# Transformer block with causal attention: one decision on the score bound, read at the end, in place of one for each chunk

## The chip, the cores and the metric

The kernel runs on one core of one Trainium2 chip. The metric is the time of one execution on the device in microseconds (us), the median of three runs. Engines are named as in the profile: PE is TensorE's matmul, PEld its weight load, DVE is VectorE, ACT is ScalarE, POOL is GpSimd, SP is SyncE, which here issues all DMAs.

## What is computed

One pre-norm transformer block over 2048 tokens of width 256, in float32. The attention has 16 heads of width 16 and is causal; the second half is a linear layer with a routed low-rank addition (8 experts of rank 16, the best 2 of each token).

```python
def block(x):                       # x: 1, 2048, 256
    h = layernorm(x)
    Q, K, V = h @ Wq.T, h @ Wk.T, h @ Wv.T          # 16 heads of 16
    scores = Q @ K.T / 4
    scores = where(later key, -inf, scores)
    x = x + (softmax(scores) @ V) @ Wo.T
    h = layernorm(x)
    logits = h @ gate_w.T + gate_b
    top, at = top_k(logits, 2)
    gates = softmax(top)
    return x + h @ W.T + b + sum(gates * delta[at])  # delta = (h @ A.T) @ B.T for each expert
```

## The kernel before, in words

The tokens are cut into 16 tiles of 128 (`TILES`) and 4 chunks of 512 (`NCHUNK`, four tiles each). Attention goes through the chunks of queries in order. Within a chunk it goes through four quads of heads (`i`). The work is cut into 272 units (`UNITS`): a unit is the transposed scores of two heads (one bank for each) of one block of 128 keys against up to 512 queries, 1024 columns in all. ACT takes the exponential of a unit in one instruction (L846), without subtracting a row maximum; that is allowed as long as a bound on the scores holds. A chunk c has 8c+5 units for each quad, so the chunks have 20, 52, 84 and 116.

TensorE multiplies exponentials by values in groups (`GROUPS`, 160 of them): a group is one block of keys for the four heads of a quad, four matmuls side by side into the one bank `acc`, which is summed over all groups of the quad. After a quad's last group DVE copies `acc` out (`keep_sums`, L1067), and the next quad's first group waits for that copy (`acc_read`).

Three buffers limit how far the engines run apart. There are 3 score buffers (`BANKS`), so the scores of unit u wait for the exponential of u-3. There are 8 buffers for exponentials (`PROBS`), so the exponential of u waits until the values have used unit u-8 (`pv_done`, L845). There is one bank `aux` for all other matmuls.

The order is written out by hand in steps. Step s issues on PE the scores of units 2s and 2s+1 (L741), then a piece, then the groups due at this step (L758), then in chunk 0 a second piece. `steps_of_groups` sets when a group is due: two steps after its last unit, and the first group of a quad one step later still. A unit is at least partly above the diagonal in a quad's last five units; DVE clears the later keys there (`clear_later_keys`, L1062) after the exponential and before the values.

A piece (`place_pieces`) is one link of the chain of another tile: `turn_x`, `project_qk` and `project_v` prepare the tiles of the next chunk; `turn_sums`, `turn_back`, `o`, `turn_y`, `ffn`, `turn_gated` and `lora` finish a tile of an earlier chunk. Each waits for the reader of the piece before it, since all write `aux`. The last four tiles are finished after the loop (`TAIL_ORDER`).

The bound: for each chunk DVE squares the rounded queries and keys, two pieces (`norm_q`, `norm_k`, L624) sum the squares by head, DVE takes the maximum of each (L993) and decides in seven short instructions (`decide_bound`, L1006 to L1019) whether the scores stay small, written to `is_bounded[0, c]`. For chunk 0 that stands in `project_first_chunk`, ahead of the first scores; there PE also turns tile 4 (L604) only after `norm_read`.

At the start of each chunk PE, DVE and SP load `is_bounded[0, c]` into a register and branch on it. PE has the chunk's steps twice, once for each outcome, and so passes two branches in a row. With the inputs here the bound always holds, so the second copy and the shifts on DVE are always jumped over.

SP stores and reloads the split queries and keys of the next chunk through DRAM (`store_parts`, `load_queries`, `load_keys`): 16-bit halves, stacked by head. Before scores of a chunk start, PE waits for `stack_in`.

## Time and profile before

| what | value |
|---|---|
| median of 3 runs | 413.61 us (411.25 to 413.66) |
| the profiled execution, whole | 415.72 us |
| its span, first to last instruction | 413.9 us |
| mean granted clock of TensorE | 0.95 |
| PE busy | 363.4 us, 88% |
| ACT busy | 279.8 us, 68% |
| DVE busy | 213.3 us, 52% |
| bound for the chunk 0 decided, first scores | 22.9 us, 24.15 us |

The profile is of one execution. A busy time is the sum of an engine's instructions; an idle time stands at the instruction that ended it, with what released it ("issue" means that the profile shows nothing it waited for).
### The profile page before, as it was taken

The numbers are of one execution on the slowest core, as the hardware profiler recorded it, in microseconds if no ns is written. First come the engines' busy times: TensorE is split into PE (matmuls) and PEld (weight loads), VectorE is DVE, ScalarE is ACT, GpSimd is POOL, SyncE is SP. The second block draws the span as 40 slices with busy tenths as digits, with TensorE's granted clock in tenths as the row PEclk, the third lists the DMA queues.
The fourth block names the chain that finished last, engine by engine and source line by source line (L and its number), as shares of the span: only waits on it lengthen the run. The fifth ranks groups of instructions, "written<-read, shape, count | busy, mean of one in ns | idle before, by whom it ended". The sixth has DMA issues, their size and how long they took to land.

```text
span 413.9 us, 7036 instructions
## 1 busy us (share of the span) xinstructions
PE 363.4 (88%) x2558; PEld 142.1 (34%) x2558; DVE 213.3 (52%) x734; ACT 279.8 (68%) x317; POOL 47.8 (12%) x75
## 2 busy tenths in 40 slices
PE   7966975899998799999999979998997999797884
PEld 3544621445332254423323223233322323211542
DVE  4647565354766535555555444546446344402385
ACT  2524345767887777788788856888787588799121
POOL 5000100001011100011121111211121111100050
PEclk9988869899999999999999999999999899899896
DMA  6578335022350021261000000000000000000001
GB/s 197 159 253 258 82 103 157 18 60 78 89 169 13 3 53 51 74 194 52 14 1 15 13 5 13 2 14 0 14 13 2 13 2 13 14 0 4 3 1 51
DMA packets 29390, 23.51 MB, mean 57 GB/s; under 512 B 15392, under 2 KB 25888, under 8 KB 29344
## 3 DMA queue, kind: packets, MB, share of 16 engines
q1 hardware_dynamic: 29344, 22.91, 18.6%
q8 instruction: 28, 0.46, 0.5%
q14 instruction: 18, 0.15, 0.1%
HBM read 12.41 MB, written 10.49 MB: 55 GB/s over the span
## 4 chain that ended last, share of the span: by engine, by line
PE 63%; DVE 18%; issue 8%; ACT 8%; POOL 2%; DMA 1%; ACTq 0%; DVEq 0%
PE acc L758 23%; PE scores L741 12%; PE aux L612 7%; ACT probs L846 7%; PE aux L669 5%; PE aux L653 3%; PE aux L682 2%; DVE probs L1062 2%; PE aux L618 2%; PE aux L638 1%; DVE ffn L1109 1%; POOL exp_gap L1217 1%; DVE parts L977 1%; DVE gates L1137 1%; PE aux L661 1%
## 5 line engine op out<-in xcount | busy, mean ns | idle before, releaser
L846 ACT ACTIVATE probs<-scores 128x1024 f32<-128x1024 f32 x272 | 260.5, 1031 | 86.1 <-PE scores L741 74.9
L758 PE MATMUL acc<-probs,v_aug 128*32 128x512 f32 (+3 forms) x1280 | 149.5, 555 | 3.3 <-DVE probs L1062 2.4
L741 PE MATMUL scores<-q_stack,k_stack 64*128 64x512 f16 (+3 forms) x640 | 87.3, 357 | 15.6 <-issue 12.1
L741 PEld LDWEIGHTS scores<-q_stack,k_stack 64*128 64x128 f16 x640 | 21.1, 95 | 116.5 <-ACT probs L846 78.8
L1062 DVE TENSOR_TENSOR probs<-probs,masks_sb 128x512 f32<-128x512 f32 (+1 forms) x80 | 44.2, 579 | 23.9 <-ACT probs L846 23.3
L758 PEld LDWEIGHTS acc<-probs,v_aug 128*32 128x32 f32 x1280 | 31.8, 111 | 54.6 <-issue 34.9
L612 PE MATMUL aux<-xT,wqkv_sb 128*128 128x128 f32 x192 | 28.8, 311 | 1.0 <-DVE xT L964 1.0
L612 PEld LDWEIGHTS aux<-xT,wqkv_sb 128*128 128x128 f32 x192 | 26.4, 221 | 5.7 <-issue 3.2
L975 DVE CAST parts<-qk 128x512 f16<-128x512 f32 x12 | 5.1, 427 | 39.9 <-ACT qk L838 39.9
L1206 POOL TENSOR_TENSOR rstd<-ve,minus_half 128x1 f32<-128x1 f32 x12 | 7.3, 608 | 112.2 <-DVE ve L955 112.2
L669 PE MATMUL aux<-wffn_sb,yT 128*128 128x392 f32 x48 | 20.0, 543 | 0.0
L1211 POOL TENSOR_TENSOR rstd<-ve,minus_half 128x1 f32<-128x1 f32 x12 | 6.6, 549 | 106.3 <-DVE ve L1093 106.3
L1109 DVE COPY ffn<-aux 128x392 f32<-128x392 f32 x12 | 6.8, 567 | 22.8 <-PE aux L669 22.8
L1086 DVE TENSOR_TENSOR y<-aux,x_sb 128x256 f32<-128x256 f32 x12 | 5.1, 425 | 23.9 <-PE aux L653 23.9
L1217 POOL TENSOR_TENSOR exp_gap<-euler,top_gap 128x1 f32<-128x1 f32 x12 | 6.6, 550 | 90.3 <-DVE top_gap L1122 90.3
L1067 DVE COPY sums<-acc 128x512 f32<-128x512 f32 x16 | 11.0, 687 | 10.3 <-PE acc L758 10.2
L618 PE MATMUL aux<-wqkv_sb,xT 128*128 128x256 f32 x48 | 13.6, 405 | 1.2 <-ACT qk L838 1.0
L1159 DVE TENSOR_TENSOR result<-aux,yb 128x256 f32<-128x256 f32 x12 | 5.1, 425 | 17.7 <-PE aux L682 17.7
L1098 DVE TENSOR_SCALAR yln<-y,mv,rstd 128x256 f32<-128x256 f32 x12 | 9.7, 810 | 8.0 <-POOL rstd L1211 8.0
L653 PE MATMUL aux<-wo_sb,attn_t 128*128 128x256 f32 x48 | 13.6, 405 | 0.0
L838 ACT COPY qk<-aux 128x512 f32<-128x512 f32 x12 | 7.0, 585 | 9.4 <-PE aux L612 9.4
L676 PE MATMUL aux<-ident_sb,gated 128*128 128x128 f32 x12 | 3.9, 326 | 9.1 <-DVE attn_t L1080 8.2
(148 smaller groups left out, 328.1 us busy)
## 6 DMA issues: line engine op xcount, KB each, us to landing
q_stack<-q_dram SPq DMA_DIRECT2D x32, 128.0 KB, 2.8
k_stack<-k_dram SPq DMA_DIRECT2D x32, 128.0 KB, 2.8
qk_dram<-qk SPq DMA_DIRECT2D x12, 256.0 KB, 2.5
x_sb<-x SPq DMA_DIRECT2D x3, 512.0 KB, 6.8
q_dram<-parts SPq DMA_DIRECT2D x12, 128.0 KB, 2.0
k_dram<-parts SPq DMA_DIRECT2D x48, 32.0 KB, 1.9
out<-result SPq DMA_DIRECT2D x12, 128.0 KB, 1.7
qk_dram<-probs SPq DMA_DIRECT2D x4, 256.0 KB, 3.4
```

What stands on the lines that cost most here:

```text
L612: m = pe.matmul(aux[:, n * P:(n + 1) * P], wqkv_sb[:, k, col:col + P], xT[:, k, :], start=(k == 0), stop=(k == KH - 1))
L618: m = pe.matmul(aux[:, 0:D], xT[:, k, :], wqkv_sb[:, k, 2 * D:3 * D], start=(k == 0), stop=(k == KH - 1))
L653: m = pe.matmul(bank_of(g)[:, 0:D], w.attn_t[:, k, :], wo_sb[:, k, :], start=(k == 0), stop=(k == KH - 1))
L669: m = pe.matmul(bank_of(g)[:, 0:FFN], w.yT[:, k, :], wffn_sb[:, k, :], start=(k == 0), stop=(k == KH - 1), skip_group_check=True)
L741: m = pe.matmul(to, k_stack[row:row + STACK, kb // TPC, 2 * i + p, kb % TPC * P:(kb % TPC + 1) * P], q_stack[row:row + STACK, c % 2, 2 * i ...
L758: m = pe.matmul(acc[32 * hp:32 * hp + 32, lo:CHUNK], v_aug[:, kb, QUAD * i + hp, :], probs[:, u % PROBS, hp % 2, col:col + CHUNK - lo], st ...
L846: act.activation(probs[:, u % PROBS], scores[u % BANKS][:], ACT.Exp, scale=EXP_SCALE).then_inc(exp_done, 1)
L1062: dve.tensor_tensor(tile, tile, mask, ALU.min).then_inc(causal_done, 1)
L1067: dve.tensor_copy(sums[:, c % 3, i, :], acc[:]).then_inc(acc_read, 1)
L1098: dve.tensor_scalar(w.yln, w.y, w.mv2[:, 0:1], w.rstd2, ALU.subtract, ALU.mult).then_inc(yln_ready, 1)
L1109: dve.tensor_copy(w.ffn, bank_of(g)[:, 0:FFN]).then_inc(ffn_ready, 1)
L1217: pool.tensor_tensor(w.exp_gap, euler[:], w.top_gap, ALU.pow).then_inc(gap_exp, 1)
```

## The change

There is one decision for the whole kernel instead of four. `norm_q` and `norm_k` of chunk 0 become pieces like the others, behind the projections of chunk 1; the decision is made once, after `norm_k` of chunk 3. The steps run without any load or branch. At the very end PE, ACT, DVE, POOL and SP each load the one result and branch: if the bound does not hold, a general path in compact loops computes the attention again and overwrites the output. With the inputs here it is jumped over.

A group of values is now due three steps after its last unit, and the extra step ahead of a quad's first group is gone. `squares` has two buffers. The mask loaded from DRAM has one plane instead of two, and the semaphores and buffers of the old general path are gone.

```diff
-        s = max(s, (last_unit(g) + 4) // 2 + (1 if g.first else 0))
+        s = max(s, (last_unit(g) + 6) // 2)
...
-            pre += [("norm_q", c + 1), ("norm_k", c + 1)]
             if c == 0:
                 pre.remove(("turn_x", TPC))
+                pre += [("norm_q", 0), ("norm_k", 0)]
+            pre += [("norm_q", c + 1), ("norm_k", c + 1)]
...
-        squares = sb("squares", [P, 2 * KH, CHUNK], BF16)
+        squares = sb("squares", [P, 2, 2 * KH, CHUNK], BF16)
...
                 pe.wait_ge(consts_in, 16 * 2)
-                pe.wait_ge(squared, 2 * KH)
-                pe.wait_ge(first_qk32_ready, 2)
-                for a in range(2):
-                    sum_squares(0, a, first_banks[a])
-                pe.wait_ge(norm_read, 1)
+                pe.wait_ge(first_qk32_ready, 1)
                 turn_x(TPC)
...
             pe.wait_ge(ones_set, 1)
-            for c in range(NCHUNK):
-                if c == 1:
+            for s in range(STEPS):
+                if s == FIRST_STEP[1]:
                     pe.wait_ge(post_weights_in, 16 * 5)
-                pe.wait_ge(bound_step, BOUND_STEPS * (c + 1))
-                bounded = pe.value_load(is_bounded[0:1, c:c + 1], min_val=0, max_val=1)
-                with pe.If(bounded == 1):
-                    for s in range(FIRST_STEP[c], FIRST_STEP[c + 1]):
-                        step(s, False)
-                with pe.If(bounded == 0):
-                    pe.wait_ge(gen_loaded[c], 16 * QUAD * (2 * c + 5))
-                    if c > 0:
-                        pe.wait_ge(exp_done, FIRST_UNIT[c])
-                    pe.wait_ge(*bank_read(*PIECE_BEFORE[PIECE_AT[FIRST_STEP[c], 0]]))
-                    row_maxima(c)
-                    for s in range(FIRST_STEP[c], FIRST_STEP[c + 1]):
-                        step(s, True)
-            for s in range(QK_STEPS, STEPS):
-                step(s, False)
+                step(s)
             pe.wait_ge(exp_done, len(UNITS))
...
+            pe.wait_ge(bound_step, BOUND_STEPS)
+            bounded = pe.value_load(is_bounded[0:1, 0:1], min_val=0, max_val=1)
+            with pe.If(bounded == 0):
+                general()
...
                 normalise_x(TPC)
-                for a in range(2):
-                    read_norm(0, a, first_banks[a])
-                decide_bound(0)
                 store_xT(TPC)
...
             def norm_k(c):
-                read_norm(c, 1, aux[:])
-                decide_bound(c)
+                read_norm(c, 1)
+                if c == NCHUNK - 1:
+                    decide_bound()
...
             for t in range(TPC):
                 store_result(TILES - TPC + t)
+            sp.wait_ge(bound_step, BOUND_STEPS)
+            bounded = sp.value_load(is_bounded[0:1, 0:1], min_val=0, max_val=1)
+            with sp.If(bounded == 0):
+                general()
             for b in range(2):
```

SP and DVE lose their loads and branches in the loop in the same way, and ACT and POOL gain the load and branch at their end.

The order on PE where chunk 0 begins. Before (`aux<-squares` are the sums of squares, `aux<-ident_sb,xln` turns tile 4, `scores<-q_stack,k_stack` are the first units):

```order
L590 MATMUL scores<-wqkv_sb,probs 128x256 x8
L624 MATMUL aux<-squares,head_sum_sb 16x512 x2
L624 MATMUL acc<-squares,head_sum_sb 16x512 x2
L604 MATMUL aux<-ident_sb,xln 128x128 x2
L778 TENSOR_LOAD is_bounded
L778 ISA x2
L779 COMPARE_AND_BRANCH
L741 MATMUL scores<-q_stack,k_stack 128x512 x4
L612 MATMUL aux<-xT,wqkv_sb 128x128 x8
```

and now:

```order
L578 MATMUL scores<-wqkv_sb,probs 128x256 x8
L588 MATMUL aux<-ident_sb,xln 128x128 x2
L696 MATMUL scores<-q_stack,k_stack 128x512 x4
L596 MATMUL aux<-xT,wqkv_sb 128x128 x8
```

The sums of squares, the load and the branch are gone from between the first chunk's values projection and the first scores. The sums stand in steps 5 and 6 of chunk 0 instead.

The order on PE where chunk 0 ends. Before, the copy for a bound that holds ends with:

```order
L741 MATMUL scores<-q_stack,k_stack 128x384 x2
L741 MATMUL scores<-q_stack,k_stack 128x128 x2
L741 MATMUL scores<-q_stack,k_stack 128x256 x4
L758 MATMUL acc<-probs,v_aug 32x256 x4
L779 UNCONDITIONAL_BRANCH
L782 COMPARE_AND_BRANCH
```

and, behind 130 rows of the other copy, chunk 1 begins:

```order
L782 UNCONDITIONAL_BRANCH
L778 TENSOR_LOAD is_bounded
L778 ISA x2
L779 COMPARE_AND_BRANCH
L741 MATMUL scores<-q_stack,k_stack 128x512 x4
L604 MATMUL aux<-ident_sb,xln 128x128 x2
L741 MATMUL scores<-q_stack,k_stack 128x512 x4
L612 MATMUL aux<-xT,wqkv_sb 128x128 x8
L758 MATMUL acc<-probs,v_aug 32x512 x4
```

Now the two chunks stand in a row:

```order
L696 MATMUL scores<-q_stack,k_stack 128x384 x2
L696 MATMUL scores<-q_stack,k_stack 128x128 x2
L696 MATMUL scores<-q_stack,k_stack 128x256 x4
L713 MATMUL acc<-probs,v_aug 32x384 x4
L713 MATMUL acc<-probs,v_aug 32x128 x4
L696 MATMUL scores<-q_stack,k_stack 128x512 x4
L588 MATMUL aux<-ident_sb,xln 128x128 x2
L713 MATMUL acc<-probs,v_aug 32x256 x4
L696 MATMUL scores<-q_stack,k_stack 128x512 x4
L596 MATMUL aux<-xT,wqkv_sb 128x128 x8
L713 MATMUL acc<-probs,v_aug 32x512 x4
```

No load and no branch is left there, and `acc<-probs,v_aug` has moved back: the last group of one quad (32x256), which stood in step 9, now stands in step 10, and the four groups of the next quad, which stood together in step 11, are spread over steps 11 and 12.

The order on PE at the last scores. Before, up to the fourth pair of branches:

```order
L741 MATMUL scores<-q_stack,k_stack 128x384 x2
L741 MATMUL scores<-q_stack,k_stack 128x128 x2
L741 MATMUL scores<-q_stack,k_stack 128x256 x4
L758 MATMUL acc<-probs,v_aug 32x512 x4
L779 UNCONDITIONAL_BRANCH
L782 COMPARE_AND_BRANCH
```

with, behind the jump, the last four groups:

```order
L758 MATMUL acc<-probs,v_aug 32x512 x4
L758 MATMUL acc<-probs,v_aug 32x384 x4
L758 MATMUL acc<-probs,v_aug 32x128 x4
L758 MATMUL acc<-probs,v_aug 32x256 x4
```

and now:

```order
L696 MATMUL scores<-q_stack,k_stack 128x384 x2
L696 MATMUL scores<-q_stack,k_stack 128x128 x2
L696 MATMUL scores<-q_stack,k_stack 128x256 x4
L713 MATMUL acc<-probs,v_aug 32x512 x12
L713 MATMUL acc<-probs,v_aug 32x384 x4
L713 MATMUL acc<-probs,v_aug 32x128 x4
L713 MATMUL acc<-probs,v_aug 32x256 x4
```

Three full groups (12 matmuls) instead of two stand behind the last scores, and no branch is between them.

## Rows read from the trace of the kernel before

**Rows 1.** The page's first part: busy us, share of the span, instructions

```profile
PE 363.4 (88%) x2558; PEld 142.1 (34%) x2558; DVE 213.3 (52%) x734; ACT 279.8 (68%) x317; POOL 47.8 (12%) x75
```

**Rows 2.** The waits: engine, line, waited for: us in all, times, longest us

```profile
PE scores L741 <- issue: 12.1, 4, 4.1
...
ACT probs L846 <- PE acc L758: 10.9, 7, 2.9
```

**Rows 3.** Stretches of the span, by engine

```profile
core 0: us, PE busy (x) PEld busy (x) DVE busy (x) ACT busy (x) POOL busy (x), PEclk, DMA share, GB/s
143.00:242.00 99.00, 96.68 (x735) 35.77 (x730) 53.07 (x183) 81.26 (x88) 11.62 (x19) 1.00 0.18 49
246.00:353.00 107.00, 100.83 (x702) 31.02 (x700) 50.80 (x193) 83.96 (x88) 16.22 (x26) 0.97 0.03 8
...
24.60:28.00 3.40, 3.40 (x17) 3.21 (x16) 0.00 (x0) 1.92 (x2) 0.00 (x0) 0.51 0.80 240
...
72.40:75.80 3.40, 3.40 (x16) 2.39 (x15) 1.09 (x5) 2.46 (x3) 0.54 (x1) 0.51 0.01 2
...
141.70:145.10 3.40, 3.40 (x26) 1.55 (x27) 1.09 (x5) 2.98 (x4) 0.55 (x1) 1.00 0.00 0
...
246.40:249.80 3.40, 3.40 (x12) 0.86 (x10) 1.02 (x7) 1.43 (x2) 0.00 (x0) 0.50 0.00 0
```

**Rows 4.** The source lines of the load, the two branches and DVE's branch

```profile
L778 PEldq TENSOR_LOAD <-is_bounded x4: 298/312/500, 23.0 to 244.6; - x4
...
L779 PEldq COMPARE_BRANCH  x4: 80/80/95, 23.9 to 245.2; - x4
...
L782 PEldq COMPARE_BRANCH  x4: 3294/3485/4160, 66.4 to 379.6; - x4
...
L1190 DVEq COMPARE_BRANCH  x4: 56/59/67, 24.7 to 242.3; - x4
```

**Rows 5.** Timeline, 12 to 32 us, and the landing times of k_stack

```profile
17.03 1.97 SPq L457 DMA_DIRECT2D k_stack<-k_dram  x4
...
20.01 0.41 DVE L959 TENSOR_SCALAR xln<-x_sb,mv,rstd 128x256 f32<-128x256 f32 x1 [0.67 <-POOL rstd L1206]
...
21.07 0.44 PE L604 MATMUL aux<-ident_sb,xln 128*128 128x128 f32 x2 [0.72 <-DVE norms L993]
...
24.15 0.71 PE L741 MATMUL scores<-q_stack,k_stack 64*128 64x512 f16 x4 [2.65 <-issue]
...
DMA to landing us min/median/max: 2.7/2.9/3.8
```

**Rows 6.** Timeline: the first rows after the three chunk boundaries

```profile
72.00 2.85 ACT L846 ACTIVATE probs<-scores 128x1024 f32<-128x1024 f32 x3 [3.30 <-PE scores L741]
...
142.12 3.85 ACT L846 ACTIVATE probs<-scores 128x1024 f32<-128x1024 f32 x4 [2.59 <-PE scores L741]
...
245.46 0.61 PE L741 MATMUL scores<-q_stack,k_stack 64*128 64x512 f16 x4 [2.86 <-issue]
```

**Rows 7.** Timeline, 372 to 392 us: the last groups of values

```profile
379.89 1.06 PE L758 MATMUL acc<-probs,v_aug 128*32 128x512 f32 x8
...
382.29 0.69 DVE L1062 TENSOR_TENSOR probs<-probs,masks_sb 128x512 f32<-128x512 f32 x1 [0.22 <-ACT probs L846]
...
383.36 4.67 PE L758 MATMUL acc<-probs,v_aug 128*32 128x512 f32 x32 [2.40 <-DVE probs L1062]
```

**Rows 8.** All the sums of squares, from the groups by line

```profile
L624 PE MATMUL aux<-squares,head_sum_sb 128*16 128x512 bf16 x14 | 5.0, 447 | 2.9 <-DVE v_aug L988 2.9
```

**Rows 9.** Timeline: an exponential that waited for values, and the projection behind it

```profile
103.45 1.02 ACT L846 ACTIVATE probs<-scores 128x1024 f32<-128x1024 f32 x1 [1.72 <-PE acc L758]
...
105.01 1.13 PE L618 MATMUL aux<-wqkv_sb,xT 128*128 128x256 f32 x4 [0.28 <-ACT qk L838]
```

**Rows 10.** The page's fifth part: the copy of the sums

```profile
L1067 DVE COPY sums<-acc 128x512 f32<-128x512 f32 x16 | 11.0, 687 | 10.3 <-PE acc L758 10.2
```

**Rows 11.** Timeline, 388 to 414 us: the last stores

```profile
409.40 2.71 SPq L484 DMA_DIRECT2D out<-k_stack  x4
```

More of the change, by code:

```diff
@@ L505, in store_shifts @@
[L505 to L513 removed]
+                sp.dma_start(gen_band, band).then_inc(gen_band_in, 16)
@@ L1202, in _ @@
+            bounded = dve.value_load(is_bounded[0:1, 0:1], min_val=0, max_val=1)
+            with dve.If(bounded == 0):
+                general()
         @block.gpsimd
@@ L1274 @@
         "expert_ids": np.broadcast_to(np.arange(E, dtype=np.float32)[None], (P, E)).copy(),
-        "ones": np.ones((1, NQUAD, S), np.float32),
+        "band": np.where(np.arange(2 * S - P)[None, :] - (S - P) <= row[:, None], BIG, -BIG).astype(np.float32),
     }
```

568 lines of the change are left out of this document (287 added, 281 removed).

## Prediction

> **What bounds the kernel now.** I read the busy shares first: PE is busy for 88% of the span, ACT for 68% [rows 1]. A share is a mean over stages, so the stretches come next. Between 143 and 242 us PE is busy for 96.68 of 99.00 us and ACT for 81.26; between 246 and 353 us PE is busy for 100.83 of 107.00 [rows 3]. There the order of work on PE is the time: whatever leaves PE, or fills an idle time of PE, moves the end. Then the waits: the longest idle time of PE is 12.1 us before L741, in only 4 places, released by "issue" [rows 2], so nothing computed was being waited for. The timeline puts them at the first scores of the four chunks: 2.65 us at 24.15 [rows 5], 2.86 at 245.46 [rows 6] and, behind the other two, ACT stands idle for 3.30 and 2.59 us waiting for scores [rows 6].
>
> What is being done there, the source lines tell [rows 4]. The branch at a chunk's start, which falls through (L779), takes 80 ns. The branch that jumps over the copy for the general path (L782) takes 3294 to 4160 ns, four times: after chunks 0, 1, 2 and also after chunk 3. Its last one starts at 379.6, so it ends at about 383; the values that wait at 383.36 behind 2.40 us of idle time [rows 7] are put down to DVE's last clearing, which ended at 382.98. But the first group there needs only earlier units, and groups before it ended at 380.95. I take these 2.40 us as a fifth boundary, made by the branch. DVE's branch over its compact body takes 59 ns [rows 4]: it is the length of the jump that costs, not the branch.
>
> The Trainium skill has two rules on this, and they disagree on what the change gives. Advanced Engine Details and Errata (Control Flow Timing) gives some 108 ns for a compare-and-branch; by that the five places would give back half a microsecond in all. Runtime: NRT & Kernel Launch (Instruction fetch mechanics) says that a taken branch to a target outside the fetched pages stalls for the fetch; by that the places give back what L782 takes. The trace agrees with the second for L782 and with the first for L779 and L1190.
>
> **The change part by part.** The sum is made against the profiled execution, 415.72 us with a span of 413.9; the median of the runs, 413.61, is 2.1 us lower, and I apply the same difference to it.
>
> Head. Before, PE turned tile 4 at 21.07 after the norms, then waited for the bound and the load, and began at 24.15 [rows 5]. Now the tile can be turned when xln is written, 20.42, and the scores wait for k_stack: four DMAs issued from 17.03 to 19.00, the last at about 18.6, landing 2.9 us later at 21.4 (at worst 3.8, 22.4) [rows 5]. First scores at 21.5: gain 2.6, between 1.7 and 3.1.
>
> Boundaries. After chunk 0, ACT was idle 3.30 us; PE's idle time was longer (4.1, the longest in rows 2), but the third and fourth unit's scores wait for exponentials there, so I take ACT's: 3.3. After chunk 1 ACT's 2.59, of which I take 2.5; after chunk 2 PE's 2.86, taken as 2.9 [rows 6]. Sum 8.7. Lower bound 5: at each, a wait for an exponential or for DVE's clearing might stand behind the branch for 1.2 us. Upper bound 9.5. What is late next: the scores of chunk 1 need reloaded keys, whose DMAs shift earlier with the head, since they start from the projection of tile 7.
>
> End. A full group takes 1.06 us [rows 7]. From 379.89 on, PE now has three full groups (383.07) and the short ones, 384, 128 and 256 columns or 1.5 groups, 1.6 us: 384.7. The last clearing ends at 382.98, in time for the last group. Before, the same point was 383.36 + 4.67 = 388.03 [rows 7]. Gain 3.3, between 2.4 and 3.6. The lag of three steps adds a group behind the last scores, but it fills time in which PE waited for the last exponentials anyway.
>
> Clock. Right after the first and the third boundary PE ran 3.40 us without a gap at a granted clock of 0.5; after the second it did not fall [rows 3]. At full clock the same work takes 1.7 us. Without the idle times ahead of them, at least 3.30 and 2.86 us, I expect both stretches to go: 2 x 1.5 = 3.0, between 0 and 3.4. The stretch at 24.60 [rows 3] follows a head in which PE still does little, so I keep it. TensorE: Matmul & The Clock Gate (the HAM clock gate) in the Trainium skill ties the half clock to idleness before it; the rows agree for two boundaries and not for the second.
>
> Norm pieces. Four matmuls of sums move from the head into steps 5 and 6 of chunk 0. All 14 take 5.0 us [rows 8], so four take 1.4, on PE's path: cost 1.4, between 0 (chunk 0 is full of small waits that may cover them) and 3.
>
> Values a step later. PE's work is the same; three things change. (a) The exponential of u waits for the values of u-8. Counted from the tables, the group that it needs stands in the same step as its own scores for 8 units before and for 61 now. (b) A quad's first group stands right behind the last group of the one before, and `acc` must be copied between: 0.69 us [rows 10] plus some 0.2 of waiting on both sides, while scores (0.61 [rows 6]) and mostly a piece (0.44 or more [rows 5]) cover it; 15 times. (c) Waits of the values for fresh exponentials and clearings go, but none of the rows that I read shows one on PE besides the end's. For (a) the trace has the pattern: ACT waited 7 times, 10.9 us [rows 2], once for 1.72 us at 103.45, and PE behind it, at a projection that needs an ACT copy queued behind that very exponential, lost 0.28 us [rows 9]. ACT has 18 us of slack in 99 [rows 3]. I take 1.2 us for all of (a) to (c), between -1 and 6.
>
> Loop body on DVE and SP. Three decisions of seven short instructions and the loads leave DVE, which is idle half the time [rows 1]: 0, between -0.5 and 0. The extra fill of the small mask: 0.
>
> New end. After the last store SP loads and branches. The load to the branch took 23.0 to 24.0 on PE [rows 4], and the stores are issued until 412.1 [rows 11], so SP is through at 413.2, before the last landing at 413.9; the general paths are now short enough to jump like DVE's. Cost 0, at most 3.3, the least that a long jump takes [rows 4], if one engine's at the end is one.
>
> Sum: -2.6 - 8.7 - 3.3 - 3.0 + 1.4 + 1.2 = -15.0. That is 400.7 us for a profiled execution and 398.6 for the median.
>
> **The rivals.**
> Serial ACT and PE (the slower side). If each of the 53 new same-step dependencies cost PE what ACT waited less the one exponential it is ahead, 10.9/7 - 1.02 [rows 2, 9] = 0.54 us, that is 28.6 us: 398.6 + 28.6 = 427. It decides from 0.28 us each, where it eats the whole gain. For it: the last quad has 11 such steps in a row, and ACT is the bound there. Against it: the loss of 0.28 behind a wait of 1.72, and that two steps of PE (groups, scores, pieces) with even the shortest pieces take 2 x (0.61 + 1.06 + 0.44) = 4.2 us, and the loop of two exponentials, half the scores, a piece and a group takes 2 x 1.02 + 0.3 + 0.44 + 1.06 = 3.8.
> The boundaries were cover. What stood behind the branches (exponentials, clearings, landing keys) takes half of it, and the half clock comes elsewhere: -2.6 - 5 - 2.4 + 0 + 1.4 + 1.2 = -7.4, so 406. For it: the scores behind a boundary do need the last exponentials ahead of it, and the clock did not follow the gaps at the second boundary.
> The stall stays, since the change doesn't remove what made it: gain only the head less the norms and the lag, about 0: 413.6. The skill's 108 ns rule would be this case. Against it: L782's 3.3 to 4.2 us are in the records.
>
> **How the numbers follow.** Forecast 0.68, half the gain 0.18, no change 0.08, serial 0.06. A measurement of this kernel tells about 1% from no change, 4.1 us. Faster by over 1% (below 409.5) takes the forecast, and all but a little of the second: 0.85. Within 1%: 0.10. Slower: 0.05. The range: the terms' bounds in the good direction, not all at once, give 394; the second rival's 406 is near the other end. I take 394 to 405.5.
>
> **What would show it.** Right: no PE idle time of over 2 us between 30 and 360 us at a chunk's first scores; first scores at about 21.5; full clock behind the boundaries of chunks 1 and 3; "ACT waits for PE acc" grows from 7 to tens of times while PE's idle time does not; the last value group ends about 15 us before its 388.03; the tail from there to the end stays 26 us long. Wrong: PE idle at L758 released by DVE's copy of the sums; PE waiting for ACT at scores in the last quad, with exponentials no longer back to back; a long gap of one engine at the end; chunk 1's first scores released by a DMA.

## The result, and the profile after

The changed kernel takes 393.45 us, the median of four runs (392.62 to 394.21). The kernel before takes 412.71, the median of the three runs above and one more beside the changed kernel. The ratio is 0.9536, with a 95% interval from 0.9495 to 0.9576, so the change takes off 19.3 us. Runs more than 1.5% above the fastest of their kernel are left out of a ratio, which concerns three of ten runs in two of the experiments below. Measured once more later, next to three other kernels, it took 394.35 us (six runs, 393.13 to 395.14) against 413.08: ratio 0.9539 [0.9499, 0.9580].

Forecast were 398.6 us, in a range from 394.0 to 405.5. The direction is right; the time lies 0.55 us outside the range, on the fast side. The gain was foretold as 15.0 us and is 19.3. The later measurement, 394.35, lies just inside the range, so the 0.55 us alone would say little; that the gain is 4 to 5 us larger than the sum stands in both.

The profiled execution of the changed kernel took 394.21 us, with a span of 392.4 and a mean granted clock of 0.988. Two lines of its page, from the first part, which answers to [rows 1], and the second:

```profile
PE 350.8 (89%) x2558; PEld 135.4 (34%) x2558; DVE 210.3 (54%) x711; ACT 279.7 (71%) x317; POOL 47.6 (12%) x75
...
PEclk8999999999999999999999999999999999999997
```

The number of matmuls is what it was, 2558, but PE is busy for 350.8 us in place of 363.4. This is the first line to stop at: an engine that does the same work in 12.6 us less did it at another speed. ACT's busy time did not move (279.7 against 279.8).

The waits (engine, line, what it waited for: us in all, times, longest us), which answer to [rows 2]:

```profile
ACT probs L814 <- PE acc L713: 31.3, 39, 1.9
...
PE aux L657 <- DVE attn_t L1027: 9.7, 11, 1.9
...
PE aux L602 <- ACT qk L806: 6.6, 5, 2.5
```

"PE scores <- issue: 12.1, 4, 4.1" is gone; 0.51 us of it is left, at the first scores of the kernel. ACT's waits for values grew from 7 to 39 places and from 10.9 to 31.3 us, as the prediction said they would. PE pays for some of them at L602, in `project_v`: three waits of 1.14 us, in chunks 1 and 2, where one of 0.28 stood before. The other two waits there are in chunk 0, and the longest, 2.5 us, is missing in the changed kernel's second profile.

The loop, cut at the first exponential of each chunk and at the end of the last values, first before and then after. The columns are the stretch, its length, the busy time of each engine (with instructions), PEclk, DMA share and GB/s:

```profile
core 0: us, PE busy (x) PEld busy (x) DVE busy (x) ACT busy (x) POOL busy (x), PEclk, DMA share, GB/s
24.60:72.00 47.40, 34.62 (x252) 19.98 (x250) 27.36 (x72) 21.45 (x24) 2.00 (x3) 0.82 0.57 172
72.00:142.10 70.10, 63.82 (x513) 27.33 (x511) 40.23 (x118) 52.12 (x56) 6.28 (x10) 0.98 0.22 63
142.10:245.90 103.80, 98.62 (x746) 36.27 (x744) 55.03 (x185) 82.91 (x89) 11.62 (x19) 1.00 0.17 47
245.90:388.00 142.10, 130.18 (x915) 38.27 (x913) 57.79 (x208) 110.50 (x116) 16.22 (x26) 0.95 0.02 8
```

```profile
23.65:63.75 40.10, 28.71 (x250) 16.05 (x248) 26.36 (x66) 21.28 (x25) 2.55 (x4) 1.00 0.65 192
63.75:130.60 66.85, 62.77 (x517) 25.86 (x519) 39.49 (x112) 52.06 (x58) 6.28 (x10) 1.00 0.27 76
130.60:233.65 103.05, 98.94 (x744) 36.33 (x737) 55.54 (x185) 83.04 (x90) 11.61 (x19) 1.00 0.17 47
233.65:366.30 132.65, 124.21 (x921) 36.36 (x919) 58.38 (x209) 110.51 (x117) 16.23 (x26) 1.00 0.02 8
```

Between these two executions (415.72 and 394.21) the head gives 0.9 us, chunk 0 7.3, chunk 1 3.3, chunk 2 0.7, chunk 3 9.5, and the tail from the last values to the end takes 0.2 more, 26.1. In each stretch the busy time of PE and its remainder, the idle time, can be read apart. In chunk 3 idle time falls by 3.5 us (11.92 to 8.44) and busy time by 6.0 (130.18 to 124.21), with a PEclk of 0.95 before and 1.00 after. That is the half clock, and it is the larger part: the kernel before ran at 0.50 in four stretches of chunk 3, at 246.4 [rows 3], at 321.5 (shown further down) and in these two, and the changed kernel in none.

```profile
355.60:359.00 3.40, 3.40 (x22) 1.18 (x14) 0.43 (x2) 1.30 (x2) 0.00 (x0) 0.50 0.02 5
382.90:386.30 3.40, 2.94 (x12) 0.66 (x12) 0.09 (x1) 0.00 (x0) 0.00 (x0) 0.50 0.03 5
```

Rows of the timeline after (start, duration, engine, line, what, and in brackets the idle time before it and what ended it), which answer to [rows 5], [rows 9] and [rows 7]:

```profile
22.30 0.41 PE L588 MATMUL aux<-ident_sb,xln 128*128 128x128 f32 x2 [1.18 <-DVE xln L936]
23.22 0.61 PE L696 MATMUL scores<-q_stack,k_stack 64*128 64x512 f16 x4 [0.51 <-issue]
...
68.36 1.02 ACT L814 ACTIVATE probs<-scores 128x1024 f32<-128x1024 f32 x1 [1.72 <-PE acc L713]
...
69.92 1.13 PE L602 MATMUL aux<-wqkv_sb,xT 128*128 128x256 f32 x4 [1.14 <-ACT qk L806]
...
351.57 13.02 ACT L814 ACTIVATE probs<-scores 128x1024 f32<-128x1024 f32 x14
...
362.21 4.08 PE L713 MATMUL acc<-probs,v_aug 128*32 128x512 f32 x48
```

The bound no longer stands ahead of the first scores; they begin 0.9 us earlier than before (24.15) here, and at 21.75 in the changed kernel's second profile. Near the end ACT runs 14 exponentials back to back, the last ones of the loop among them. The last values follow without an idle time where 2.40 us stood [rows 7], and end at 366.29, that is 26.1 us before the end, while before it was 25.9. At 68.36 and 69.92 is the new chain: an exponential 1.72 us late, ACT's copy queued behind it, and PE's projection 1.14 us late behind the copy. The same pattern before cost PE 0.28 us [rows 9].

The new end (L761 loads the flag, L762 branches):

```profile
L762 PEldq COMPARE_BRANCH  x1: 233/233/233, 389.3 to 389.3; - x1
...
L761 PEldq TENSOR_LOAD <-is_bounded x1: 720/720/720, 388.2 to 388.2; - x1
```

It lies beside the last stores, and the tail is 0.2 us longer than before.

### The profile page after: what moved, and what is told of

It reads as the page before. It is cut to its first block, busy times and chain, and to the rows that moved or that the text cites. A ratio compares the mean times of both kernels' runs of the same rounds, so it can differ in the third digit from the quotient of the medians.

```text
span 392.4 us, 6977 instructions
## 1 busy us (share of the span) xinstructions
PE 350.8 (89%) x2558; PEld 135.4 (34%) x2558; DVE 210.3 (54%) x711; ACT 279.7 (71%) x317; POOL 47.6 (12%) x75
## 4 chain that ended last, share of the span: by engine, by line
PE 61%; DVE 20%; SPq 5%; issue 5%; ACT 4%; DMA 3%; POOL 2%; DVEq 0%; ACTq 0%
PE acc L713 24%; PE scores L696 11%; PE aux L596 5%; PE aux L651 4%; PE aux L637 3%; ACT probs L814 3%; PE aux L662 2%; PE aux L602 2%; DVE ffn L1055 2%; DVE probs L1010 2%; POOL exp_gap L1216 2%; DVE gates L1083 2%; PE aux L623 1%; DMA wqkv_sb<-wqkv 1%; SPq L455 1%
## 5 line engine op out<-in xcount | busy, mean ns | idle before, releaser
L713 PE MATMUL acc<-probs,v_aug 128*32 128x512 f32 (+3 forms) x1280 | 146.5, 538 | 0.8 <-DVE sums L1015 0.8
L696 PE MATMUL scores<-q_stack,k_stack 64*128 64x512 f16 (+3 forms) x640 | 85.1, 349 | 1.8 <-issue 0.5
L1010 DVE TENSOR_TENSOR probs<-probs,mask_sb 128x512 f32<-128x512 f32 (+1 forms) x80 | 44.8, 578 | 25.3 <-ACT probs L814 25.1
L713 PEld LDWEIGHTS acc<-probs,v_aug 128*32 128x32 f32 x1280 | 29.1, 108 | 41.5 <-issue 23.9
L596 PE MATMUL aux<-xT,wqkv_sb 128*128 128x128 f32 x192 | 24.6, 281 | 0.7 <-DVE xT L941 0.7
L596 PEld LDWEIGHTS aux<-xT,wqkv_sb 128*128 128x128 f32 x192 | 22.3, 191 | 4.7 <-issue 2.8
L602 PE MATMUL aux<-wqkv_sb,xT 128*128 128x256 f32 x48 | 13.6, 405 | 6.8 <-ACT qk L806 6.6
L651 PE MATMUL aux<-wffn_sb,yT 128*128 128x392 f32 x48 | 19.0, 518 | 0.0
```

Source lines behind the costliest of these rows:

```text
L596: m = pe.matmul(aux[:, n * P:(n + 1) * P], wqkv_sb[:, k, col:col + P], xT[:, k, :], start=(k == 0), stop=(k == KH - 1))
L602: m = pe.matmul(aux[:, 0:D], xT[:, k, :], wqkv_sb[:, k, 2 * D:3 * D], start=(k == 0), stop=(k == KH - 1))
L651: m = pe.matmul(w.bank[:, 0:FFN], w.yT[:, k, :], wffn_sb[:, k, :], start=(k == 0), stop=(k == KH - 1), skip_group_check=True)
L696: m = pe.matmul(scores[u % BANKS][:, j, col:col + n], k_stack[row:row + STACK, kb // TPC, 2 * i + p, kb % TPC * P:(kb % TPC + 1) * P], q_s ...
L713: m = pe.matmul(acc[32 * hp:32 * hp + 32, lo:CHUNK], v_aug[:, kb, QUAD * i + hp, :], probs[:, u % PROBS, hp % 2, col:col + CHUNK - lo], st ...
L1010: dve.tensor_tensor(tile, tile, mask, ALU.min).then_inc(causal_done, 1)
```

## The experiments

Twelve measurements were made, in three sets of four, each set next to new runs of the kernel before. Theory 1 is the prediction's mechanism: the long jump at four chunk ends, the idle time it makes on PE, and the half clock that follows that idle time. The question was which of its terms was too small.

### The branches alone

From the kernel before, the branches, the loads of the flag and all the general path are taken out; the bound is still decided per chunk, chunk 0's ahead of the first scores, and the values stand at their old step.

```diff
-                bounded = pe.value_load(is_bounded[0:1, c:c + 1], min_val=0, max_val=1)
-                with pe.If(bounded == 1):
-                    for s in range(FIRST_STEP[c], FIRST_STEP[c + 1]):
-                        step(s, False)
-                with pe.If(bounded == 0):
...
+                for s in range(FIRST_STEP[c], FIRST_STEP[c + 1]):
+                    step(s, False)
```

> The kernel before without any load or branch in the loop; the bound is still decided for each chunk, and PE still waits for chunk 0's decision. The general path is left out, and never ran. Theory 1 (the far jumps cost their own time and bring half-clock stretches with them, and that is nearly all of the gain): 396 to 399 us, half-clock time in the span down from 41 us to under 20. Rival (the values a step later bring the part that the forecast missed): 400 to 402, half-clock stretches in the last two chunks stay. Rival (the jumps only cover waits): 406 or more.

Measured: 396.69 us (395.19 to 397.02), ratio 0.9592 [0.9527, 0.9657] to a before of 412.65. So 16.0 of the 19.3 us go with the loads and branches. The load and branch ahead of chunk 0's first scores are among them: the first exponential starts at 23.45 in place of 24.60, so 1.1 us of what the prediction called the head are in this number. Its stretches:

```profile
23.45:66.06 42.61, 33.89 (x254) 19.77 (x252) 26.84 (x75) 21.34 (x24) 2.55 (x4) 0.84 0.64 187
66.06:132.36 66.30, 61.90 (x510) 26.09 (x509) 40.41 (x119) 52.10 (x58) 6.27 (x10) 1.00 0.27 72
132.36:233.20 100.84, 98.53 (x746) 36.24 (x744) 54.93 (x186) 82.90 (x90) 11.61 (x19) 1.00 0.17 48
233.20:369.00 135.80, 126.24 (x915) 37.15 (x913) 58.32 (x210) 110.53 (x116) 16.21 (x26) 0.97 0.02 8
```

Chunk 1 gives 3.8 us and chunk 2 3.0, where the terms said 4.0 (2.5 and half of the clock's 3.0) and 2.9. Chunk 0 gives 4.8 where 3.3 was said, chunk 3 6.3 where 4.8 was said. The expectation's number for half clock missed: 26 us are left in the span (2 x (1 - 0.967) x 394.9). Chunk 0 still has a PEclk of 0.84, though there is no jump in it.

### The values a step later, alone

```diff
-        s = max(s, (last_unit(g) + 4) // 2 + (1 if g.first else 0))
+        s = max(s, (last_unit(g) + 6) // 2)
```

> The kernel before with the new due times of the groups only (three steps, no extra step before a quad's first group). Theory 1: the same or slower by up to 3 us (411 to 416), since ACT now waits for values in the same step 61 times. Rival (the later values bring the missed part): faster by 4 us or more, under 409.

Measured, on the kernel before: 413.96 us (ten runs, 409.64 to 416.77; 412.48 for the seven that the ratio takes), ratio 0.9991 [0.9940, 1.0042]. Alone it does nothing that can be told in the time. Its profile has both sides of it: chunk 2 takes 106.0 us in place of 103.8, and chunk 3 takes 138.1 in place of 142.1, with 3.4 us at half clock where the kernel before had 13.7.

### Everything but the later values

The same line the other way round, in the changed kernel.

> The changed kernel with the old due times of the groups. Theory 1: 391 to 394.5 us, no slower than the changed kernel's 393.45, because the branches are what went. Rival (later values): 397 to 400, with half-clock stretches back around 320 and 355 us.

Measured: 394.13 us (393.17 to 394.80), ratio 0.9545 [0.9481, 0.9608]. By these medians the later values are worth 0.7 us, within the spread. Against the kernel without branches, this one differs by the head and the place of the sums of squares: 396.69 - 394.13 = 2.6 us, where the prediction's two terms were 2.6 and 1.4 the other way, 1.2 net; and since 1.1 us of the head went with the branches, only 0.1 was left to expect. The two intervals overlap widely, so the difference is not resolved.

### The kernel before, once more

A control: the unchanged kernel under a name of its own, for the granted clock of more executions than one.

> The kernel before once more, for the granted clock of several executions. Theory 1: mean clock 0.94 to 0.96 in all of them, against 0.98 to 0.99 of the changed kernel. Rival (the clock of the one profiled execution was bad luck): some executions of before at 0.97 or more, and their times lower by the half of the stretches that they lack.

Measured: 413.83 us (ten runs, 409.34 to 417.73; 413.65 for the seven that the ratio takes), ratio 1.0000 [0.9955, 1.0044]. The medians of this kernel in the five measurements on record lie between 412.65 and 413.83, its single runs between 409.34 and 417.73. The expectation on the clock was too narrow: the mean clocks of the ten executions run from 0.943 to 0.975, and the fastest execution is the one at 0.975. In the 46 executions of this kernel that ran beside the experiments the median is 0.962, which is 31 us of half clock, so the profile that the prediction rests on, with 0.950 and 41 us, is one of the low ones.

### Four far jumps put back

The changed kernel, in which PE loads a constant flag at the end of each chunk and jumps over 700 matmuls, which never run.

```diff
+SKIPPED = 700
...
+                if s in FIRST_STEP[1:]:
+                    flag = pe.value_load(flag_cell[0:1, 0:1], min_val=0, max_val=1)
+                    with pe.If(flag == 0):
+                        for _ in range(SKIPPED):
+                            pe.matmul(aux[:, 0:P], ...)
```

> The changed kernel with a load and a branch on PE alone put back ahead of the first step of chunks 1, 2 and 3 and ahead of the last values; each branch jumps over 700 matmuls that never run, and there is no wait for a bound. Theory 1 (the far jump is the price): PE idle 2.2 to 3.5 us at each of the four places, branch records over 3 us, half-clock stretches back behind one or more of them; 404 to 409 us. Rival (the load and the wait for the bound were the price, not the jump): under 398.

Measured: 415.12 us (ten runs, 412.20 to 417.81), ratio 1.0036 [0.9999, 1.0072]. The whole gain is gone; theory 1 had expected 404 to 409 and was too low by 6 us at least.

### Four near jumps

The same with 20 matmuls to jump over in place of 700.

> The same, but each branch jumps over 20 matmuls. Theory 1: branch records of 0.05 to 0.25 us, PE loses at most the load, 0 to 1 us at each place: 393.5 to 397 us. Rival (any branch or load drains PE's queue and costs the same): as far_jumps, 404 or more.

Measured: 395.41 us (393.40 to 397.86), ratio 0.9548 [0.9483, 0.9612], 2.0 us above the changed kernel's 393.45, 1.1 above its 394.35, and as theory 1 said. In the profiles the near jumps cost 0.3 us up to the last values (345.20 against 344.95 in the changed kernel's second profile, shown last); 1.0 us more lies at the very end, a tail of 27.1 us in place of 26.1, with the far jumps too, and no run shows why. The source line of the branch (ns min/median/max), and the row that sums four stretches from the first exponential to the last values, for the far and then for the near jumps:

```profile
L760 PEldq COMPARE_BRANCH  x4: 3274/3582/4152, 62.8 to 379.3; - x4
...
sum 363.90, PE 326.22 PEld 118.42 DVE 180.05 ACT 267.40 POOL 36.71; mean PE 81.55 PEld 29.60 DVE 45.01 ACT 66.85 POOL 9.18
```

```profile
L760 PEldq COMPARE_BRANCH  x4: 205/210/243, 63.5 to 363.7; - x4
...
sum 345.20, PE 316.08 PEld 114.88 DVE 179.77 ACT 266.99 POOL 36.70; mean PE 79.02 PEld 28.72 DVE 44.94 ACT 66.75 POOL 9.18
```

This is the cleanest reading of the case, since the two programs differ in nothing that runs. The far one takes 18.7 us more between these points. Its matmuls are the same, and PE is busy for 10.1 us more (326.22 - 316.08); idle time accounts for the other 8.6 (37.7 against 29.1). So a far jump costs 4.7 us in these two executions: 2.1 of idle PE, and 2.5 of matmuls that run slower. The sum of 4.7 holds, since the medians (415.12 and 395.41) give 4.9. The split is less sure, for not all of the half clock lies behind a jump. The far kernel has two stretches of 3.4 us at half clock ahead of its first jump that the near one lacks, and one at 322.8 with no jump near. Behind the jumps themselves stand 13.7 us at half clock, after the first (66.8), the second and the third, and none after the fourth; they are worth at most half of that, 1.7 us a jump. The second and the third:

```profile
138.50:141.90 3.40, 3.40 (x15) 0.67 (x15) 1.09 (x5) 1.64 (x2) 0.55 (x1) 0.50 0.00 0
244.30:251.10 6.80, 5.57 (x16) 1.54 (x16) 1.45 (x10) 1.02 (x1) 0.14 (x1) 0.50 0.01 2
```

Chunks 1 to 3 alone take 15.2 us longer with far jumps, 8.1 of it idle time and 7.1 slower matmuls. Over all executions of the two kernels the mean clocks give 33 and 13 us at half clock (medians), so at most 10 of the 19.7 us between the medians are the clock's. About half and half is what the runs bear out. The timeline shows both at the first jump: 4.13 us of idle time, and the four score matmuls behind it take 1.04 us in place of 0.61.

```profile
67.07 1.04 PE L698 MATMUL scores<-q_stack,k_stack 64*128 64x512 f16 x4 [4.13 <-issue]
```

The Trainium skill, Runtime: NRT & Kernel Launch (Instruction fetch mechanics), has a taken branch to a target outside the fetched pages wait for the fetch. These records agree: 0.21 us near, 3.3 to 4.2 us far, with the same flag and the same branch. The DMA queue of the instructions agrees too, first with far and then with near jumps (packets, MB, share of 16 engines):

```profile
q8 instruction: 28, 0.46, 0.5%
```

```profile
q8 instruction: 22, 0.36, 0.4%
```

In the far trace one packet of 16384 bytes starts inside each of the four branch records, 0.9 to 1.7 us after its start (64.4, 135.0, 242.8 and 380.2 us). In the near trace one of the four records has a packet beside it, and that branch took 0.21 us all the same.

### Matmuls that fill the idle time

The kernel before, with twelve unused matmuls of 512 columns issued at the end of each chunk, just ahead of the jump.

```diff
+                    for _ in range(FILL):
+                        pe.matmul(aux[:], ident_sb[:].bitcast(BF16)[:, 0:P], k_stack[:, 0, 0, :].bitcast(BF16),
+                                  start=True, stop=True)
```

> The kernel before with 12 matmuls of 512 columns into the unused bank aux ahead of each of its four far jumps (2.6 us of work at full clock that nobody reads; a wait for the last piece's reader is added), so that PE is busy while its sequencer is stalled. Theory 1 (the idle time brings the half clock): PE's idle time at the boundaries shrinks to under 1.5 us, the half-clock stretches right behind them go, and the time falls by 2 to 5 us though the jumps stay: 408 to 411. Rival (the clock falls whatever PE does there): 412 to 416.

Measured: 410.19 us (408.74 to 411.67), ratio 0.9916 [0.9883, 0.9949]: 2.9 us less, with more work in it. The jumps still take 3.3 to 4.05 us each. Two of its stretches, chunks 1 and 3:

```profile
69.05:139.50 70.45, 64.93 (x524) 27.41 (x523) 40.23 (x118) 52.09 (x56) 6.29 (x10) 1.00 0.23 63
...
244.85:381.80 136.95, 127.39 (x926) 38.04 (x925) 57.69 (x208) 110.29 (x116) 16.21 (x26) 0.99 0.03 8
```

PEclk rises from 0.98 to 1.00 in chunk 1 and from 0.95 to 0.99 in chunk 3, and chunk 3 is 5.1 us shorter though its record holds 11 matmuls more. The stretches at half clock that stood behind the first, the third and the fourth jump of the kernel before are gone, with the jumps still there. So at these places PE's idle time brought the half clock, and not the branch as such. The 5.1 us of chunk 3 are not all the filling's, since the stretch at 355.6 is missing too and stood behind no jump; and chunk 2, which had no half clock to lose, takes 1.5 us more for it.

### Nine buffers for exponentials

The changed kernel with `PROBS` 9 in place of 8 (the squares of chunk 0 move into memory that is free then). With nine, the exponential of u waits for values of an earlier step.

```diff
-PROBS = 8
+PROBS = 9
```

> The changed kernel with nine buffers for exponentials instead of eight (the squares of chunk 0 move into the third buffer of the sums to make room), so that no exponential needs values of its own step. Theory 1 (the lag's cost is the same-step dependency, paid in chunks 1 and 2): ACT's waits for values fall from 31 us to under 5, chunk 2 gets 1.5 to 2.5 us shorter, 391 to 392.5 us in all. Rival (the cost is the copy between a quad's last and the next one's first group): 393 to 394.5, as the changed kernel.

Measured: 390.27 us (388.32 to 392.02), ratio 0.9423 [0.9367, 0.9480], a little better than expected in the whole; chunk 2 gained less than the 1.5 to 2.5 us expected. The waits, and chunks 1 and 2:

```profile
ACT probs L816 <- PE scores L698: 64.8, 85, 3.3
...
PE aux L604 <- ACT qk L808: 1.3, 2, 0.7
```

```profile
62.80:126.05 63.25, 61.75 (x511) 25.44 (x510) 39.44 (x113) 52.12 (x57) 6.29 (x10) 1.00 0.27 76
126.05:227.85 101.80, 98.59 (x746) 35.84 (x744) 55.25 (x187) 83.27 (x88) 11.61 (x19) 1.00 0.17 48
```

No wait of ACT for values is left, PE's wait for the projection's copy falls from 6.6 to 1.3 us, and chunks 1 and 2 are 3.6 and 1.25 us shorter than in the changed kernel. So the wait was part of the price of the later values. It isn't all: with the old step chunk 2 takes 100.84 us with eight buffers, 1.0 less than here. This version has the lowest time of all.

### Four kernels side by side

The last set puts the changed kernel, the one with the old step of the values, nine buffers with the old step, and a price for the moved sums on one chip.

> The changed kernel as it is, once more, beside the three others of this call, so that the lag can be read from medians of one chip. Theory 1 (the prediction's 15.0 us were too small by sizes, not by this chip's spread): median 392.5 to 395, with about 9 to 15 us of half clock in the span. Rival (the first measurement of it was a lucky one): 396 to 399.

> The changed kernel with the values at their old step, once more. Theory 1 (the lag's later exponentials cost 2 to 3 us in chunks 1 and 2, and what it frees elsewhere pays for them, so that in sum it does nothing): within 1 us of the changed kernel in this call, first scores of chunk 1 to 3 about 2.7 us earlier in sum in these two chunks. Rival a (the prediction's: the lag costs 1.2): 1 to 1.5 us below the changed kernel. Rival b (the lag gains): 1 us or more above it.

> Nine probability buffers and the values at their old step. The ninth buffer gave 3 us with the later values, since then no exponential waits for values of its own step. Theory 1 (the two need each other: with the old step eight buffers are already enough, so the ninth adds nothing to it): 393 to 395, the same as with eight. Rival (the ninth buffer helps by itself, because it lets ACT run ahead over PE's pieces): 390 to 391.5, as with the later values, and then the lag is worth nothing at all.

The fourth computes the sums of squares of chunk 0 three times over:

```diff
-                for k in range(KH):
+                for k in list(range(KH)) * (3 if c == 0 else 1):
```

> The changed kernel, where the sums of squares of chunk 0 are each computed three times over: eight matmuls of 512 columns more, in steps 5 and 6 of chunk 0. At 0.21 us each with the full clock to 0.38 as recorded that is 1.7 to 3.0 us of PE work more. Theory 1 (the prediction's term of 1.4 for four of them was wrong since chunk 0 has 11 us of PE idle time that they fill): up to 0.7 us over the changed kernel, and chunk 0's idle time of PE shorter by what the matmuls take. Rival (they stand on PE's path, as the prediction said): 1.7 to 3.0 us over it.

Measured, against a before of 413.08 us:

| kernel | median of 6, us | ratio, 95% |
|---|---|---|
| changed kernel | 394.35 (393.13 to 395.14) | 0.9539 [0.9499, 0.9580] |
| old step of the values | 394.36 (392.23 to 395.58) | 0.9543 [0.9498, 0.9589] |
| nine buffers, old step | 392.34 (391.49 to 396.12) | 0.9509 [0.9460, 0.9558] |
| sums of chunk 0 three times | 397.08 (395.34 to 398.50) | 0.9606 [0.9561, 0.9651] |

The changed kernel's time came out as expected, but not its clock: its profiled execution has 23 us of half clock (mean clock 0.971) where 9 to 15 were expected, and its six executions lie between 5.5 and 23 us. The slowest and the fastest of them differ by 17 us of half clock and only 2.0 us of time.

The later values do nothing in sum (394.35 and 394.36), as theory 1 said. The old step's stretches show why, chunk by chunk:

```profile
22.00:62.75 40.75, 29.24 (x258) 16.62 (x256) 26.47 (x66) 21.43 (x24) 2.55 (x4) 1.00 0.64 190
62.75:129.05 66.30, 61.89 (x510) 26.10 (x509) 39.38 (x111) 52.09 (x57) 6.27 (x10) 1.00 0.27 76
129.05:229.90 100.85, 98.55 (x746) 36.24 (x744) 54.93 (x186) 82.91 (x90) 11.62 (x19) 1.00 0.17 48
229.90:365.80 135.90, 126.39 (x915) 37.47 (x913) 58.31 (x210) 110.51 (x116) 16.23 (x26) 0.97 0.02 8
```

Chunks 1 and 2 are 0.55 and 2.2 us shorter than with the later values. These two stages repeat to 0.05 us in the three profiles of each order with eight buffers and no jumps. Chunk 3 is 3.25 us longer, and its PEclk is 0.97: two stretches at half clock, one of them here.

```profile
299.00:303.40 4.40, 2.46 (x25) 0.62 (x28) 3.31 (x11) 3.26 (x4) 0.79 (x2) 1.00 0.00 2
303.40:306.80 3.40, 3.40 (x26) 1.17 (x18) 0.69 (x1) 1.39 (x2) 0.00 (x0) 0.50 0.00 0
```

In the kernel before, the same point of chunk 3 (76 us behind its first exponential) looks the same, and no jump is near. What stands ahead of it in both is a wait of PE for `attn_t`, here of 2.29 us (1.94 in the old step's profile):

```profile
320.45 0.33 PE L676 MATMUL aux<-ident_sb,gated 128*128 128x128 f32 x1 [2.29 <-DVE attn_t L1080]
```

```profile
317.20:321.50 4.30, 2.01 (x23) 0.66 (x22) 2.96 (x9) 2.73 (x3) 0.26 (x1) 1.00 0.01 2
321.50:324.90 3.40, 3.40 (x28) 1.11 (x21) 0.69 (x1) 1.52 (x2) 0.00 (x0) 0.50 0.00 0
```

With the later values and eight buffers neither stretch was there in both profiles of the changed kernel, and that is what pays for chunks 1 and 2. But it isn't certain in either order: one profile of the old step had none of it (and a chunk 3 of 132.9 us), and the kernel with the sums three times over had the first. The wait ahead of it is there in every profile, 1.9 to 2.3 us long. Over all fourteen profiles, the seven with the old step have ten such stretches in the middle of chunk 3 and the seven with the later values three. So it is a tendency in these profiles, not something shown.

The ninth buffer: with the later values 390.27, with the old step 392.34. Theory 1 for the latter (no gain over eight buffers) looks wrong by 2.0 us, and the rival (all of nine's gain) by 2.1 the other way; the intervals [0.9367, 0.9480] and [0.9460, 0.9558] barely overlap. Chunks 1 and 2, which have no half clock in either, settle more than the medians. With nine buffers and the old step they are:

```profile
65.40:129.60 64.20, 61.75 (x510) 26.09 (x509) 39.80 (x111) 51.88 (x58) 6.26 (x10) 1.00 0.24 69
129.60:230.45 100.85, 98.55 (x746) 36.25 (x744) 54.96 (x186) 82.69 (x90) 11.62 (x19) 1.00 0.17 48
```

So the ninth buffer takes 2.1 us off the old order's chunk 1 (66.30 to 64.20) and nothing off its chunk 2: theory 1 was wrong. And with nine buffers the later values gain 0.95 us in chunk 1 (63.25) and lose 0.95 in chunk 2 (101.80), nothing in sum. What else parts 390.27 from 392.34 lies in the chunks where the half clock changes from execution to execution (3.4 us of it in chunk 3 with the later values, 6.8 with the old step), or in the chips, since the two ran in different sets.

The sums: eight more matmuls in chunk 0 cost 2.7 us by the medians, 0.34 each, as the rival said. The six runs of this kernel (395.34 to 398.50) and those of the changed one (393.13 to 395.14) don't overlap, so most of the added work is on PE's path. The line's record and chunk 0 of that kernel:

```profile
L608 PE MATMUL aux<-squares,head_sum_sb x24: 379/382/634, 52.6 to 168.1; 128*16 128x512 bf16 x24
```

```profile
22.20:65.85 43.65, 33.56 (x258) 18.60 (x256) 26.47 (x67) 21.29 (x25) 2.55 (x4) 0.92 0.65 192
```

My expectation that chunk 0's idle time would hide them was wrong by the times; the stretch itself can't show it, since PE's idle time in it, 10.1 us, lies between the changed kernel's two (11.4 and 7.8). The changed kernel's second profile warns against reading chunk 0 from one execution alone:

```profile
22.20:64.50 42.30, 34.48 (x250) 19.65 (x248) 26.22 (x65) 21.25 (x24) 2.55 (x4) 0.84 0.63 187
...
234.45:367.15 132.70, 124.23 (x921) 36.37 (x919) 58.44 (x209) 110.55 (x117) 16.21 (x26) 1.00 0.02 8
```

The same program had a PEclk of 1.00 in chunk 0 in one execution and 0.84 in the other, and PE was busy 5.8 us longer, but the chunk took only 2.2 us longer: the other 3.6 us came out of waits. In chunk 3 the two agree within 0.05 us.

## Why the prediction was right in its mechanism and too small in its sum

By medians the gain of 19.3 us splits so: 16.0 for the loads and branches (foretold 16.1: the three terms of 15.0 and the 1.1 us of the head that went with them), 2.6 for the rest of the head and the moved sums (foretold 0.1), 0.7 for the later values (foretold -1.2). The misses of 2.5 and 1.9, less 0.1, make the 4.3. Both are smaller than one interval, so it is the profiles and the clocks of the executions that tell where they come from.

**The jump.** Right. The record of L782, not the Trainium skill's 108 ns for a compare-and-branch (Advanced Engine Details and Errata, Control Flow Timing), was the price. The branches' terms (boundaries 8.7, end 3.3, clock 3.0) add up to 15.0, 16.1 with the load in the head; without the branches alone 16.0 us go [interval 14.2 to 19.5 from the ratio's]. As a whole well sized, though not in its parts. Chunks 1 and 2 came out within 0.2 us of their terms.

**Boundary 1.** "[...] so I take ACT's: 3.3" was the first undersized step. PE's idle time there was 4.1, and PE sets the time. In the kernel without branches chunk 0 gave 4.8. How much of the rest is its erratic clock can't be said from one profile of each.

**Clock.** This is the step that failed: "I expect both stretches to go: 2 x 1.5 = 3.0, between 0 and 3.4". The term counts the two stretches of 3.40 us right behind the boundaries and puts the rest of the half clock at nothing, without a reason, though it was there to be read: the mean clock of 0.950 makes 41 us (2 x 0.05 x 413.9), and the windows at 38.2, 55.3, 321.5, 355.7 and 383.3 of the profile before show 0.50 or 0.51 each. So 3.4 was no upper bound. Chunk 3 of the kernel before had about 14 us of it (2 x 0.05 x 142.10), of which the stretch at 246.4 that I counted is 3.40; three more stand at 321.5, 355.6 and 382.9, the last of them behind the idle time I had priced as "the end". PE's busy time in chunk 3 fell by 6.0 us where my term put 1.5 there.

Over all executions the mean clocks give these medians of half clock: 31.2 us in the kernel before (46 executions beside the experiments), 23.7 without branches (4), 19.6 in the changed kernel with the old step (10) and 14.9 in the changed kernel (10). So 16 us of it went, worth at most half of that, 8 us, where the term had 3.0; that is up to 5 us more than the sum had, against the miss of 4.3. Only 7.5 of the 16 us went with the branches, worth at most 3.8, and for them the term was sized about right. The other 9 went with the moved sums and the later values, to which the prediction gave no share of the clock at all. How much of them those two changes cause stays open: the ranges of these executions overlap (22.8 to 26.1, 10.2 to 26.0, 5.5 to 22.8 us), and one us of half clock is worth less than half a us where waits take it up (17 us of it were worth 2.0 between two executions of the changed kernel). The far and near jumps show the cause, not that split: with nothing else changed, half clock went from 13 to 33 us.

**End.** Right in kind. Idle time of PE in chunk 3 fell by 3.5 us for the term of 3.3, and 2.40 us of idle time had stood behind the branch; the tail stayed at 26.1 us, as said. The other signs came too: no long idle time of PE at a chunk's first scores, full clock behind the boundaries, ACT's waits for values in tens of places.

**Head.** The first exponential was 2.4 to 2.6 us earlier in eight of the nine profiles with the new head (22.0 to 22.2 against 24.6), as the term of 2.6 said; in the one taken right after the prediction it was at 23.65. That execution had a PEclk of 0.86 in its first 12 us (1.00 in the second profile), and its first cast of queries began at 12.55 against 10.94, so this is the clock once more and not the head's order. The kernel before did the same: its second profile has 0.86 there, the first cast at 12.41, and the first exponential at 26.4 in place of 24.6.

**Norm pieces.** Right by the medians. Four matmuls at 0.34 are 1.4 us, the term's own value.

**Values a step later.** "I take 1.2 us" failed in its sign only on the sum: the loss is there and larger than I said (0.55 and 2.2 us in chunks 1 and 2, where the sum had 1.2 in all). The chain named, ACT's wait, its copy, the projection, is 1.14 us of the 2.2 in chunk 2; the rest has no one wait behind it. But chunk 3 gave it back, with less half clock in these profiles. In the medians it is 0.0 (394.35 and 394.36).

**The rivals.** Serial ACT and PE (427) is out: ACT's waits did grow to 39 places and 31.3 us, but chunks 1 and 2 pay 2.8 us for it, not 28.6. Its last quad, where I saw its best case, ran with exponentials back to back. "The boundaries were cover" is out too: they gave more than their idle time. "The stall stays" is out: the changed kernel has no jump on PE over 0.23 us. The branch at the end (up to 3.3) is 0.23 us, hidden but for the 0.2 us of the tail.

What stays open: why 2.6 us and not 0.1 stand between the kernel without branches and the one with head and sums moved. Their median half clock differs by 4 us, worth at most 2, but each interval is some 2.6 us wide to either side, so it may be spread alone.

## What to carry to other kernels

A taken jump over a long body costs its engine microseconds even if the body never runs: price it from the branch's own record, put rare code where no jump over it lies on the common path, and decide once at the end if the common result can be computed anyway. Then price the clock with the idle time: compare PE's busy time for equal numbers of matmuls, and count all time at half clock, in more executions than the profiled one, not just the stretches beside the gap in question. When consumers move later, count buffers again: with eight, the exponential waited for values of its own step, and one buffer more was worth 3 to 4 us (2 with the old step).

## What the runs showed of the hardware

- A branch on PE took 0.21 us over 20 matmuls and 3.3 to 4.2 us over 700, with the same flag and form. On PE that left 2.6 to 4.1 us of idle time.
- A far jump cost 4.7 us by the profiles and 4.9 by the medians. About half is idle time of PE; the rest is matmuls at half clock, of which on average at most 1.7 us a jump lie right behind it. Twelve unused matmuls ahead of each of four jumps took 2.9 us off the kernel.
- A packet of 16384 bytes on the instruction queue starts within each far branch's record.
- Idle time of 2 us and more on PE does not always bring half clock. The changed kernel had such gaps at 33.9 (2.58 us), 40.6 (2.47) and 51.4 (2.08) with PEclk 1.00 throughout chunk 0; its second profile had 2.58 and 2.08 at the same places and a PEclk of 0.84. What decides between the two, no run here tells.
- The stages without half clock repeat from execution to execution to 0.05 us (chunk 2 at 100.84, 100.85 and 100.84 in three profiles of the old step; 103.06, 103.11 and 103.09 in three of the later one), while the whole differs by some us. A difference of 0.5 us can be read from such a stage, not from medians.
